# Per-tile signals for the normalised rows, and the expert counts moved behind one matmul block, in a two-layer gated transformer kernel

## The reference, cut to what matters

```python
x = x + tanh(g_xattn[0]) * L0_xattn(layernorm(x), ctx)    # relu attention without softmax
x = x + tanh(g_ffn[0])   * L0_ffn(layernorm(x))           # 256 -> 1024 -> 1024 -> 256, weights of +1 or -1
x = x + tanh(g_xattn[1]) * L1_xattn(layernorm(x), ctx)    # 16 heads, shared keys, softmax
x = x + tanh(g_ffn[1])   * L1_ffn(layernorm(x))           # 64 experts, top 8, 128 slots each, and a shared expert

def layernorm(x):
    m, v = mean(x, -1), var(x, -1)
    return (x - m) / sqrt(v + 1e-5)

# in L1_ffn: the slot of a token in an expert is how many earlier tokens chose that expert
onehot = one_hot(e_flat, 64)
pos = cumsum(onehot, axis=0) - 1
kept = pos < 128
```

## Time and profile before

| | |
|---|---|
| median of 3 runs | 1893.12 us |
| lowest and highest of them | 1881.17 and 1898.27 us |
| the profiled execution | 1875.85 us |
| its span, from first to last instruction | 1874.1 us |
| mean granted TensorE clock | 0.974 |
| PE busy with matmuls | 1693.0 us, 90% of the span, 17308 matmuls |
| DVE busy | 1322.2 us, 71% |
| ACT busy | 986.2 us, 53% |
| POOL busy | 945.9 us, 50% |

### The profile page before, as it was taken

How to read it: one execution, slowest core, us unless ns; L and a number is a source line. 1 busy time by engine, 2 the same in 40 slices (tenths; PEclk the granted TensorE clock), 3 DMA queues, 4 the chain that set the end, 5 groups by cost and what they waited for, 6 DMA issues and landing times.

```text
span 1874.1 us, 51360 instructions
## 1 busy us (share of the span) xinstructions
PE 1693.0 (90%) x17308; PEld 1427.9 (76%) x17308; DVE 1322.2 (71%) x4639; ACT 986.2 (53%) x2819; POOL 945.9 (50%) x1507
## 2 busy tenths in 40 slices
PE   3799999999999999999999999999999998448886
PEld 2588888888888888888888888888888876347775
DVE  5467777777777777777777777777777776436564
ACT  2355555555555555555555555555555554214443
POOL 2114555555555555555555555555555554344554
PEclk8899999999999999999999999999999999679999
DMA  7401111111000001000000000000000012128886
GB/s 222 142 9 50 44 40 37 41 41 35 25 24 22 25 20 31 30 21 21 24 27 22 27 20 20 13 22 24 23 19 19 21 50 73 47 85 207 200 201 137
DMA packets 102657, 101.12 MB, mean 54 GB/s; under 512 B 38880, under 2 KB 92074, under 8 KB 102617
## 3 DMA queue, kind: packets, MB, share of 16 engines
q1 hardware_dynamic: 68824, 81.43, 14.1%
q0 software_dynamic: 33792, 19.17, 5.8%
HBM read 51.63 MB, written 111.84 MB: 87 GB/s over the span
## 4 chain that ended last, share of the span: by engine, by line
PE 47%; issue 15%; DVE 12%; POOL 8%; DMA 8%; ACT 8%; SPq 0%; POOLq 0%; DVEq 0%; ACTq 0%
PE bank L1081 14%; PE bank L990 8%; DMA out<-ey,aid 7%; POOL table L615 5%; PE ps_lg L1139 4%; ACT p L802 3%; PE ps_tr L1012 3%; PE ps_yo L1095 3%; PE ps_yo L990 3%; PE ps_pt L1154 3%; PE bank L1067 3%; PE ps_m L990 2%; ACT xr L741 2%; POOL rs L631 1%; DVE pt_l L1630 1%
## 5 line engine op out<-in xcount | busy, mean ns | idle before, releaser
L615 POOL DMA_INDIRECT table<-xs,slot x496 | 504.1, 1016 | 200.8 <-issue 171.8
L802 ACT ACTIVATE p<-ps_lg,rmax 128x77 f32<-128x77 f32 x1024 | 235.6, 349 | 140.4 <-DVE rmax L1625 136.7
L557 POOL TENSOR_TENSOR pool_pad<-pad_in 128x1 f32<-128x1 f32 x352 | 67.9, 193 | 399.8 <-PE ps_lg L1139 171.2
L1081 PE MATMUL bank<-h_h,held 128*128 128x256 f16 x2048 | 265.9, 273 | 4.1 <-DVE h_l L1560 2.0
L1081 PE MATMUL bank<-h_l,held 128*128 128x256 f16 x2048 | 265.4, 273 | 0.0
L1081 PEld LDWEIGHTS bank<-h_l,held 128*128 128x128 f16 x2048 | 200.3, 98 | 23.8 <-issue 0.6
L1081 PEld LDWEIGHTS bank<-h_h,held 128*128 128x128 f16 x2048 | 193.1, 98 | 27.6 <-DVE h_l L1560 2.6
L631 POOL TENSOR_TENSOR rs<-nt,minushalf 128x2 f32<-128x2 f32 x128 | 92.9, 726 | 200.6 <-DVE nt L1525 192.1
L1560 DVE SCALAR_TENSOR_TENSOR h_l<-bank,h_h 128x512 f16<-128x512 f32 x256 | 175.1, 684 | 11.8 <-ACT h_h L783 7.0
L1625 DVE TENSOR_REDUCE rmax<-ps_lg 128x8 f32<-128x616 f32 x128 | 101.7, 795 | 83.6 <-PE ps_lg L1139 82.5
L706 POOL DMA_INDIRECT out<-ey,aid x64 | 98.7, 1542 | 99.1 <-DVE aid L1898 67.0
(11 more groups left out here) (277 smaller groups left out, 4611.6 us busy)
## 6 DMA issues: line engine op xcount, KB each, us to landing
ew<-in_e_wts SPq DMA_DIRECT2D x48, 384.0 KB
table<-xg SPq DMA_DIRECT2D x8, 1284.0 KB, 16.7
xg<-table SPq DMA_DIRECT2D x64, 160.5 KB
xs<-xr SPq DMA_DIRECT2D x31, 320.0 KB, 2.6
x<-in_x SPq DMA_DIRECT2D x32, 256.0 KB
out<-x SPq DMA_DIRECT2D x32, 256.0 KB
table<-xs,slot POOLq DMA_INDIRECT x496
held<-in_e_wts SPq DMA_DIRECT2D x16, 384.0 KB, 4.6
```

The costliest lines, as they stand in the source:

```text
L615: g.indirect_dma_start(out=table, out_offset=bass.IndirectOffsetOnAxis(ap=slots[:, t, k:k + 1], axis=0), in_=rows[:, t, :], in_offset=None ...
L802: ins = a.activation(p32[:, h * S2:(h + 1) * S2], ps_lg[:, h // HB, h % HB * S2:(h % HB + 1) * S2], ACT.Exp, bias=rmax[r % 2][:, h:h + 1])
L1081: ins = mm(two(bank[j % 2])[:, m % 2, :], wb1[:, k, m * P:(m + 1) * P], hp[:, k, :], start=(i == 0 and k == 0), stop=(i == 1 and k == FK - 1))
```

## The change: what it does

It has two parts.

1. For norms 1, 2 and 3 each of the two activations raises `ln_nm[i]`, which so counts tiles, two a batch. PE waits in `transposes` for the first tile ahead of the first two transposes, and for the second ahead of the other two. Everything else that waits for these semaphores waits for twice the count: `pass_rows` on SyncE, and `ln_sums`, `a_x1` and `b_x2` on DVE. Norm 0 stays as it was, with one signal a batch.
2. On PE, `d_cp(d)` stands behind `b_l1(3, n)`, not ahead of it. DVE's order is unchanged.

```diff
             def pass_rows(b):
                 sp.wait_ge(ch_ok, b + 1)
-                sp.wait_ge(ln_nm[3], b + 1)
+                sp.wait_ge(ln_nm[3], 2 * b + 2)
...
                 for t in range(T2):
-                    ins = a.activation(dst[:, t, 0:D], src[:, t, :], ACT.Identity, bias=nb[i][:, t:t + 1], scale=rs[i][:, t:t + 1])
-                ins.then_inc(ln_nm[i], 1)
+                    a.activation(dst[:, t, 0:D], src[:, t, :], ACT.Identity, bias=nb[i][:, t:t + 1],
+                                 scale=rs[i][:, t:t + 1]).then_inc(ln_nm[i], 1)
...
-                pe.wait_ge(ln_nm[i], b + 1)
-                for t in range(T2):
+                for t in range(T2):
+
+                    if i > 0:
+                        pe.wait_ge(ln_nm[i], 2 * b + t + 1)
+                    elif t == 0:
+                        pe.wait_ge(ln_nm[i], b + 1)
                     for c in range(C2):
                         ins = nc.tensor.transpose(two(ps_turned[i])[:, c, t * P:(t + 1) * P], src[:, t, c * P:(c + 1) * P], ident[:, :])
                 ins.then_inc(tr_rdy[i], 1)
...
                     c_pt(2, c)
                     c_pt(3, c)
+                if on(n):
+                    b_l1(3, n)
                 if on(d):
                     d_cp(d)
-                if on(n):
-                    b_l1(3, n)
                 if on(c):
                     c_av(1, c)
                     c_lg(3, c)
...
-                w(dve, ln_nm[i], b)
+                w(dve, ln_nm[i], b if i == 0 else 2 * b)
...
-                w(dve, ln_nm[1], b)
+                w(dve, ln_nm[1], 2 * b)
...
-                w(dve, ln_nm[2], b)
+                w(dve, ln_nm[2], 2 * b)
```

## The result

The changed kernel takes **1871.76 us** (median of 7 runs, 1867.36 to 1874.24), the kernel before, run beside it, 1888.96 us (median of 7, 1881.17 to 1898.27). The ratio is 0.9912, with a 95% interval of 0.9888 to 0.9937: 0.9% less time. The forecast was 1878.5 us, 0.8% less, between 1862 and 1897.

The account below looks back on a forecast made before the run. PE was taken to bound the loop, with only its idle time, some 3% at most, to win. Gains of 0.235 us at transposes 3 and 2, 0.47 a body over 31 bodies, gave 1893.12 - 14.6 = 1878.5 us, range 1862 to 1897.

Parts of the forecast that it names:

- The two places and their sum: PE's waits at the norm 3 and norm 2 transposes: both gains kept, 0.47 us a body, 14.6 us over 31 bodies.
- Transposes 3: Norm 3 transposes on PE: first pair starts on tile 0, second at 800.48 as before; gain 0.235 us a body.
- Transposes 2: Norm 2 transposes on PE: first pair follows `d_gu(2)` without a wait, second without a gap; gain 0.235 us a body.
- DVE's and SyncE's waits change only in their number: Waits of DVE and SyncE for the norm signals, whose counts double: taken to add no cost.
- The added waits of PE: Three more waits a body on PE at the transposes: costed at nothing, with 0.42 us a body as upper bound.
- Transposes 1: Norm 1 transposes on PE: no wait now, so no gain; insurance against ACT being late.
- Rival D: Each new PE wait costs a handoff even when met: 0.42 us against 0.47, 1.5 us left, 1891.6 us; chance 0.08.
- Part 2: Counts `d_cp` moved behind `b_l1(3)`: gain 0, bounds 0 and 0.07 us a body, as `c_lg(3)` waits for ACT anyway.
- The first chip's body: Sign in the profile after: the loop body takes 48.07 us, not 48.54.
- rival B: After transposes 2 the ACT, DVE and argmax chain becomes later; half given back, 7.3 us left, 1885.8 us; chance 0.14.
- Rival C: Late signal at DVE's argmax vanishes through small shifts in some 28 bodies: 12.3 us more, 1866 us; chance 0.14.
- Rival E: A late signal of 0.7 us strikes an added or the moved signal every body: 19.6 us lost, 1898 us; chance 0.12.

Follow-up runs that it names:

- e1: Only the tile-by-tile signals, without the move of `d_cp`, against the kernel before: 1812.72 us against 1827.58, ratio 0.9922.
- e5: The changed kernel again, unaltered, on a third chip, against the kernel before: 1813.82 us against 1828.84, ratio 0.9912.
- e11: The changed kernel again, unaltered, on a fourth chip, for its trace beside that of the kernel before: 1813.59 us (one run).
- e10: The kernel before again, unaltered, on a fourth chip, for its trace: 1828.82 us (one run).
- e7: The changed kernel without DVE's wait for the norm 2 signals ahead of the sum `b_x2`: 1811.23 us (one run).
- e2: Only the move of `d_cp` behind `b_l1(3)`, signals as before, against the kernel before: 1827.83 us, ratio 1.0000.
- e8: Tile-by-tile signals without DVE's waits for norms 1, 2 and 3, counts in front of the fourth block: 1806.51 us, ratio 0.9876 to the kernel before.
- e9: The changed kernel, counts behind the fourth block, without DVE's waits for norms 1, 2 and 3: 1807.47 us, ratio 0.9889 to the kernel before.

## Why the prediction was right

**The two places and their sum.** The step held: PE's idle time at transposes 3 and 2 reaches the end, and 0.47 us a body was forecast where the three other chips show 0.42 (e1) and 0.45 (e5, e11). 14.6 us were forecast; part 1 alone gave 14.9 on the second chip, the whole change 15.0 (e5) and 15.2 (e11 against e10, one run each). On the first chip, for which the forecast was made, the agreement is partly luck: the medians gained 17.2 us, but the traces show only half of the forecast gain in its bodies.

**The terms were off in both directions.** Transposes 3 give 0.28 us, not 0.235. The prediction kept the handoff of 0.14 us for the second pair and halved the time of the four transposes; the handoff shrinks to 0.05, and the saved pair is worth 0.19. Transposes 2 would give 0.28 as well: with the register operation out of the way, `b_l2(1)` to the end of the transposes takes 6.93 us in e7 (778.09 to 785.02), against 7.21. The changed kernel itself has 7.04 there. The sentence that failed is "DVE's and SyncE's waits change only in their number". It costs 0.10 us a body, and 0.28 + 0.28 - 0.10 = 0.46. So 0.47 came out nearly right because its errors cancel.

**The added waits of PE.** Costing them at nothing was right. Transposes 1 now hold a second wait, and their row has the same 0.60 us (at 800.84) as in the earlier trace rows, and in e7 those of norm 2 take 0.43 us with two waits, where transposes 1 took 0.44 with one before (804.01 to 804.45). Rival D is out. By the Trainium skill (Advanced Engine Details and Errata, section Miscellaneous Facts), with its 50 to 100 ns to read a semaphore from a sequencer, an estimate would make them 0.05 to 0.1 us longer each. For a wait that is already met, this trace disagrees.

**Part 2.** Nothing, as forecast (e2, and e8 against e9). The bodies of e1 and e5 are 0.04 us apart, on two chips, which is left open. The 0.07 us wait ahead of `d_cp`, which part 2 removed, exists only on the first chip. In e10 `d_cp` follows `c_pt(3)` without one:

```profile
812.85 0.38 PE L1154 MATMUL ps_yo<-ident,p 128*128 128x128 f32 x2
813.07 0.22 PE L1233 MATMUL ps_tr<-chosen,before 128*128 128x64 f16 x2
```

**The first chip's body.** It was forecast at 48.07 us and came to 48.28 (median 48.31). There 0.28 + 0.17 was won at the two transposes, and 0.10 lost at the attention's sum (0.64 to 0.74 us behind PE), 0.06 between `c_pt(3)` and `c_lg(3)` (2.88 to 2.94), and 0.05 ahead of the hot sums (0.33 to 0.38). That leaves the 0.24 us between the medians. Half is given back, as in rival B, but by signals of PE that got later (from 0.44 to 0.55 us after the matmul at the attention's sum, from 0.80 to 0.83 at the argmax), not by a chain of its own over ACT and DVE. Why they got later is not shown. Rival C's premise was right in that such a delay comes and goes, and wrong that small shifts of the program remove it: the argmax waited 0.40 us before and 0.43 after. It is missing throughout on the other chips. Rival E asked for a late signal at one of the added or moved ones; the added ones are ACT's and the moved one is `cp_rdy` of `d_cp`, and in the changed kernel's trace each comes within 0.02 us of its instruction's end (`cp_rdy` 27 times of 27; of ACT's 164 of 165 in the record).

**What the sum doesn't explain.** On the first chip the medians differ by 17.2 us, while its bodies in the profiles give 7 to 8 us, and the two profiled executions differ by 2.25. The medians agree with the other chips' ratio (0.9912 and 0.9912). That the late signals vary from run to run there would fit the kernel before's spread of 17 us against under 9 elsewhere, but the traces are of two executions only, so this is a guess.

## What to carry to other kernels

Where a consumer works tile by tile, a signal per tile is worth about one tile's work of the consumer (0.19 us here), and not the whole wait. Look in the raw records at which instruction carries the wait that ends last: here another 0.09 us hung on that. When a semaphore's count per step changes, look at every other engine that waits for it: a count that must be computed can put a register operation in front of a critical instruction, and a redundant wait is cheaper dropped than doubled (another 2.6 us in e7, and 6 to 7 in e8 and e9). Before a wait of a few tenths is priced, find out whether it is there on another chip.

## What the runs showed of the hardware

The kernel before took 1828 us on three chips and 1889 on a fourth, at the same mean granted clock (0.972 to 0.977 in its runs there, 0.974 in its profiled execution here), and at 1.00, the full 2.4 GHz, all through the loop from 217 to 1530 us. Of the 47.0 us between the profiled executions (1875.85 and e10's 1828.82), 35.7 lie in the first 29 bodies, some 1.3 us in most of them, and 12.4 in the last two (109.9 against 97.6); elsewhere 1 us goes the other way. In a body of the loop 0.46 us are lost ahead of the hot sums, behind the late argmax, 0.42 behind the attention's late sum, and 0.27 and 0.15 between the four parts of the attention. What makes PE's signals late there is open. It isn't TensorE's pace, since the matmuls keep theirs: `b_l2(1)` to the end of the transposes of norm 2 takes 7.21 us on the first chip and in e10.

A wait that rides on a register operation of DVE held the next instruction back by 0.1 us after the signal (0.13 us in e11, 0.02 in e10 and e7); the same operation behind the instruction didn't delay it. On PE a wait that is an instruction of its own put 0.135 us between signal and matmul, and a wait that the weight load carries 0.044.
